# Attention and feed-forward in one program: scores of two pairs of heads in a row, three work banks

## The reference

```python
q = (layernorm(layernorm_plain(x)) @ Wq).reshape(b, 112, 16, 64)   # then q * (1 + side) + side
k, v = split(layernorm(ctx) @ Wkv)                                  # each 375 x 16 heads x 64
attn = softmax(einsum('bihd,bjhd->bhij', q, k) / 8)
x = x + tanh(g_x) * (einsum('bhij,bjhd->bihd', attn, v).reshape(b, 112, 1024) @ Wout)
h = gelu(bitlinear(layernorm_plain(x), w1, b1))                     # bitlinear: rmsnorm, rounding to
x = x + tanh(g_f) * bitlinear(h, w2, b2)                            # 127 steps a row, ternary weights
```

## Time and profile before

| | us |
|---|---|
| median of 3 runs (1168.94 to 1169.98) | 1169.59 |
| the profiled execution | 1169.56 |
| its span | 1167.3 |
| PE busy | 1105.4 (95%) |
| ACT busy | 976.1 (84%) |
| DVE busy | 934.5 (80%) |
| POOL busy | 767.9 (66%) |

### The profile page before, as it was taken

One profiled execution on the slowest core, in us unless ns is written; L12 is line 12 of the kernel. 1 busy time (PEld: TensorE's weight loads), 2 busy tenths in 40 slices (PEclk: granted clock), 3 DMA queues, 4 the chain that ended last, 5 costly groups with the idle time before them and its releaser, 6 DMA issues.

```text
span 1167.3 us, 32324 instructions
## 1 busy us (share of the span) xinstructions
PE 1105.4 (95%) x12170; PEld 746.9 (64%) x12170; DVE 934.5 (80%) x1980; ACT 976.1 (84%) x1866; POOL 767.9 (66%) x835
## 2 busy tenths in 40 slices
...
GB/s 267 72 97 114 107 110 102 102 103 96 96 116 96 111 100 108 97 99 106 99 112 93 108 92 117 94 111 99 104 99 102 107 106 109 95 94 89 98 93 14
DMA packets 381208, 120.57 MB, mean 103 GB/s; under 512 B 354848, under 2 KB 379904, under 8 KB 381056
## 3 DMA queue, kind: packets, MB, share of 16 engines
...
...
## 4 chain that ended last, share of the span: by engine, by line
PE 76%; DVE 8%; issue 5%; ACT 4%; DVEq 3%; POOL 2%; DMA 1%; POOLq 1%; ACTq 0%
PE work L737 16%; PE work L738 15%; PE work L739 15%; PE ps_s L756 10%; PE ps_o L737 3%; PE ps_o L738 3%; PE ps_o L739 3%; PE work L819 3%; DVEq L621 2%; PE work L850 2%; PE work L844 2%; PE work L810 2%; ACT prob L520 1%; DVE qs L629 1%; DVE attn L594 1%
## 5 line engine op out<-in xcount | busy, mean ns | idle before, releaser
L361 POOL TENSOR_TENSOR pn<-prob,pn 112x750 f16<-112x750 f32 x256 | 405.0, 1592 | 213.4 <-DVE pn L667 148.4
L520 ACT ACTIVATE prob<-ps_s,neg_max 112x375 f32<-112x375 f32 x512 | 265.3, 572 | 73.0 <-DVE neg_max L660 70.4
L660 DVE TENSOR_REDUCE neg_max<-ps_s 112x2 f32<-112x750 f32 x256 | 239.4, 935 | 66.7 <-PE ps_s L756 66.7
L737 PE MATMUL work<-z,wkv_h 128*128 128x375 f16 x512 | 167.6, 327 | 7.8 <-POOL z L382 6.6
L737 PE MATMUL ps_o<-v_h,pt 128*128 128x65 f16 (+1 forms) x1536 | 164.9, 195 | 7.4 <-DMA pt<-pn 7.4
L739 PE MATMUL work<-z,wkv_l 128*128 128x375 f16 x512 | 166.4, 325 | 0.0
L738 PE MATMUL work<-z,wkv_h 128*128 128x375 f16 x512 | 166.0, 324 | 0.0
L738 PE MATMUL ps_o<-v_l,pt 128*128 128x65 f16 (+1 forms) x1536 | 165.1, 193 | 0.0
L739 PE MATMUL ps_o<-v_h,pt 128*128 128x65 f16 (+1 forms) x1536 | 164.7, 193 | 0.0
L737 PEld LDWEIGHTS ps_o<-v_h,pt 128*128 128x128 f16 (+1 forms) x1536 | 143.7, 97 | 24.2 <-DMA pt<-pn 9.2
L738 PEld LDWEIGHTS ps_o<-v_l,pt 128*128 128x128 f16 (+1 forms) x1536 | 142.8, 99 | 14.8
...
## 6 DMA issues: line engine op xcount, KB each, us to landing
...
pt<-pn SPq DMA_TRANSPOSE x256, 3.2
...
```

The lines of the kernel that those rows point to most:

```text
L361: g.tensor_tensor(pn[p % PBUF][:, 1, :, 0:SK], prob[:, p % 2], pn[p % PBUF][:, 0, :, 0:SK], ALU.subtract).then_inc(p_lo, 1)
L520: i = a.activation(prob[:, p % 2, h, :], ps_s[0:SQ, h, 0:SK], ACT.Exp, bias=neg_max[:, h:h + 1])
L660: v.tensor_reduce(neg_max[:, :], ps_s[0:SQ, 0:2, 0:SK], X, ALU.max, negate=True).then_inc(max_ready, 1)
L737: t_.matmul(dst, sh, mh, start=(n == 0), stop=False)
```

## The change

- `ps_s` has four banks, two for even and two for odd pairs; `neg_max` four columns. S of a pair waits for E of two pairs back (`exp_done >= g - 1`).
- `ps_o` has one bank, four heads at a time; `normalise_heads` runs four times an item (`N0` to `N3`), each on four heads, and `A` of every even pair waits for the last of them.
- `work` has three banks.
- The lists are new. On PE the S steps stand mostly in twos: S0 S1, S2 S3, S4 S5, S6 S7. On ACT, `GE` is followed by KH5, ZF0, SQ, ZF1 and only then E6. POOL's list is the same round, begun at another point.
- x is loaded by a step of its own, `LX`; `LD` loads ctx and, for item 1, the rest as before.
- `ot_h` and `ot_l` become one array `ot`; `pn` and `pt` are picked by the running pair number g (the same buffers, as eight pairs go round four buffers twice).

```diff
-WORK_BANKS = 4
+WORK_BANKS = 3
 ORDER["PE"] = [
-    ("K5", 0), ("K7", 0), ("V00", 0), ("A4", -1), ("S0", 0), ("V01", 0), ("A5", -1), ("V02", 0),
-    ("S1", 0), ("K0", 1), ("Q1", 0), ("A6", -1), ("S2", 0), ("OO0", -1), ("XT", -2), ("K1", 1),
-    ("A7", -1), ("K2", 1), ("V10", 0), ("ZX", 1), ("S3", 0), ("V11", 0), ("A0", 0), ("F0", -2),
-    ("K3", 1), ("S4", 0), ("OO1", -1), ("F1", -2), ("K4", 1), ("HT", -3), ("A1", 0), ("S5", 0),
-    ("WO", -1), ("V12", 0), ("Z1", 2), ("Q0", 1), ("S6", 0), ("F2", -3), ("Z0", 2), ("K6", 1),
-    ("A2", 0), ("A3", 0), ("S7", 0),
+    ("Z1", 1), ("V02", 0), ("K7", 0), ("V00", 0), ("A4", -1), ("S0", 0), ("S1", 0), ("OO0", -1),
+    ("A5", -1), ("K6", 0), ("V01", 0), ("Q1", 0), ("A6", -1), ("ZX", 1), ("S2", 0), ("S3", 0),
+    ("K1", 1), ("K0", 1), ("A7", -1), ("V10", 0), ("K2", 1), ("V11", 0), ("K3", 1), ("S4", 0),
+    ("S5", 0), ("OO1", -1), ("XT", -2), ("A0", 0), ("K4", 1), ("A1", 0), ("HT", -3), ("Q0", 1),
+    ("F1", -2), ("V12", 0), ("F0", -2), ("WO", -1), ("K5", 1), ("S6", 0), ("S7", 0), ("Z0", 2),
+    ("F2", -3), ("A2", 0), ("A3", 0),
 ]
 FIRST["PE"] = [
-    ("Z0", 0), ("Z1", 0), ("ZX", 0), ("K0", 0), ("K2", 0), ("K1", 0), ("Q0", 0), ("K4", 0),
-    ("K3", 0), ("K5", 0), ("K6", 0), ("S0", 0), ("Z0", 1), ("V00", 0), ("Z1", 1), ("V01", 0),
...
+    ("Z0", 0), ("Z1", 0), ("ZX", 0), ("K1", 0), ("K0", 0), ("K3", 0), ("K4", 0), ("K2", 0),
+    ("Q0", 0), ("Z0", 1), ("K5", 0), ("Z1", 1), ("K7", 0), ("S0", 0), ("S1", 0), ("Q1", 0),
+    ("S2", 0), ("V00", 0), ("S3", 0), ("V02", 0), ("V01", 0), ("K6", 0), ("S4", 0), ("ZX", 1),
...
 ORDER["ACT"] = [
...
+    ("PH0", 0), ("VH01", 0), ("E1", 0), ("QF1", 0), ("ZXF", 1), ("XR", -2), ("KH1", 1), ("KH0", 1),
+    ("E2", 0), ("VH10", 0), ("E3", 0), ("KH2", 1), ("PH2", 0), ("VH11", 0), ("KH3", 1), ("LNW", 2),
+    ("OH1", -1), ("E4", 0), ("KH4", 1), ("PH4", 0), ("QF0", 1), ("E5", 0), ("VH12", 0), ("GE", -2),
+    ("KH5", 1), ("ZF0", 2), ("SQ", -2), ("ZF1", 2), ("E6", 0), ("VH02", 1), ("PH6", 0), ("E7", 0),
+    ("KH7", 1), ("VH00", 1), ("HR", -2), ("OH0", 0), ("E0", 1), ("KH6", 1),
...
 ORDER["DVE"] = [
...
+    ("M0", 0), ("KL7", 0), ("VL00", 0), ("PH7", -1), ("OT0", -1), ("N2", -1), ("M1", 0), ("KL6", 0),
+    ("VL01", 0), ("PH1", 0), ("M2", 0), ("BA", 2), ("BB", 2), ("KL1", 1), ("M3", 0), ("KL0", 1),
+    ("VL10", 0), ("BS", 2), ("KL2", 1), ("N3", -1), ("VL11", 0), ("KL3", 1), ("M4", 0), ("XTE", -2),
+    ("OT1", -1), ("PH3", 0), ("KL4", 1), ("HTE", -3), ("M5", 0), ("HE1", -2), ("N0", 0), ("HE0", -2),
+    ("PH5", 0), ("VL12", 0), ("X1", -1), ("XST", -1), ("M6", 0), ("KL5", 1), ("HMX", -2), ("YE", -3),
+    ("SC1", -1), ("M7", 0), ("N1", 0), ("VL02", 1), ("SC2", -2),
 ]
 FIRST["DVE"] = [
...
+    ("BA", 0), ("BB", 0), ("BS", 0), ("WKL", 0), ("BA", 1), ("KL1", 0), ("BB", 1), ("KL0", 0),
+    ("BS", 1), ("WQL", 0), ("KL3", 0), ("KL4", 0), ("KL2", 0), ("WVL", 0), ("KL5", 0), ("M0", 0),
...
 ORDER["POOL"] = [
...
+    ("PL7", -2), ("PL0", -1), ("PL1", -1), ("ZXS", 0), ("HQ", -4), ("XQ", -3), ("QS1", -1), ("LNA", 1),
+    ("PL2", -1), ("PL3", -1), ("PL4", -1), ("PL5", -1), ("RM1", -2), ("QS0", 0), ("RM2", -3), ("ZS0", 1),
+    ("PL6", -1), ("ZS1", 1), ("XB", -2),
...
 FIRST["SP"] = [
...
+    ("LD", 1), ("LX", 1), ("LD", 2), ("LX", 2), ("T0", 0), ("T1", 0), ("T2", 0), ("LD", 3),
...
-        ps_s = st.enter_context(nc.psum_tensor("ps_s", [P, 2, HALF], F32))
-        ps_o = st.enter_context(nc.psum_tensor("ps_o", [P, 2, HALF], F32))
+        ps_s = st.enter_context(nc.psum_tensor("ps_s", [P, 4, HALF], F32))
+        ps_o = st.enter_context(nc.psum_tensor("ps_o", [P, 1, HALF], F32))
...
-                sp.dma_start(x_in[:], x[b]).then_inc(x_loaded, 16)
...
+                if name == "LX" and b > 0:
+                    sp.wait_ge(ctx_normed, b)
+                    sp.dma_start(x_in[:], x[b]).then_inc(x_loaded, 16)
...
+            def normalise_heads(b, quarter):
+                n, heads = H // 4, ps_o[0:SQ, 0, 0:4 * VW].rearrange("p (h e) -> p h e", e=VW)
+                inv = row_inv[:, n * quarter:n * (quarter + 1)]
+                dve.wait_ge(pv_done, b * PAIRS + 2 * (quarter + 1))
...
             def score(b, p):
                 g = b * PAIRS + p
-                if g > 0:
-                    pe.wait_ge(exp_done, g)
+                if g > 1:
+                    pe.wait_ge(exp_done, g - 1)
...
-                        i = t_.matmul(ps_s[0:SQ, h, 0:SK], q[r, p, :], k[r, p, :], start=(n == 0), stop=(n == 2))
+                        i = t_.matmul(ps_s[0:SQ, 2 * (p % 2) + h, 0:SK], q[r, p, :], k[r, p, :], start=(n == 0), stop=(n == 2))
...
-                if p % 4 == 0 and b * PAIRS + p > 0:
-                    pe.wait_ge(o_normed, 2 * b + p // 4)
+                if p % 2 == 0 and b * PAIRS + p > 0:
+                    pe.wait_ge(o_normed, 4 * b + p // 2)
```

More of the change, by code:

```diff
@@ L189, in build @@
         RC = IC * RING // 2
-        ot_h, ot_l = (stage[:, RC * i:RC * (i + 1)].bitcast(F16).rearrange("p (c q) -> p c q", c=IC) for i in range(2))
+        ot = stage[:, 0:2 * RC].bitcast(F16).rearrange("p (h a c q) -> p h a c q", h=2, a=2, c=IC // 2)
         x1_b2 = stage[:, 2 * RC:2 * RC + 4 * D].rearrange("p (s d) -> p s d", s=4)
@@ L219, in build @@
         q_h, q_l = sb("q_h", [P, IC, SQ], F16), sb("q_l", [P, IC, SQ], F16)
-        neg_max, row_inv = sb("neg_max", [SQ, 2]), sb("row_inv", [SQ, H])
+        neg_max, row_inv = sb("neg_max", [SQ, 4]), sb("row_inv", [SQ, H])
         prob = sb("prob", [SQ, 2, 2, SK])
@@ L360, in split_p @@
                 pool.wait_ge(p_hi_act if p in CAST_ACT else p_hi, CAST_COUNT[b, p])
-                g.tensor_tensor(pn[p % PBUF][:, 1, :, 0:SK], prob[:, p % 2], pn[p % PBUF][:, 0, :, 0:SK],
+                buf = pn[(b * PAIRS + p) % PBUF]
+                g.tensor_tensor(buf[:, 1, :, 0:SK], prob[:, p % 2], buf[:, 0, :, 0:SK],
                                 ALU.subtract).then_inc(p_lo, 1)
@@ L475, in step @@
                         act.wait_ge(full[BANK["WO", t]], USE["WO", t])
-                    a.activation(ot_h[:, 4 * half:4 * half + 4, columns(b)],
+                    a.activation(ot[:, half, 0, :, columns(b)],
                                  work[:, BANK[job], 0:4 * SQ].rearrange("p (c q) -> p c q", c=4), ACT.Identity).then_inc(o_hi, 1)
@@ L519, in step @@
                     for h in range(2):
-                        i = a.activation(prob[:, p % 2, h, :], ps_s[0:SQ, h, 0:SK], ACT.Exp, bias=neg_max[:, h:h + 1])
+                        i = a.activation(prob[:, p % 2, h, :], ps_s[0:SQ, 2 * (p % 2) + h, 0:SK], ACT.Exp, bias=neg_max[:, 2 * (p % 2) + h:2 * (p % 2) + h + 1])
                     i.then_inc(exp_done, 1)
@@ L528, in step @@
                     if g >= PBUF:
-                        act.wait_ge(turned[p % PBUF], 16 * (g // PBUF))
-                    a.activation(pn[p % PBUF][:, 0, :, 0:SK], prob[:, p % 2], ACT.Identity).then_inc(p_hi_act, 1)
+                        act.wait_ge(turned[g % PBUF], 16 * (g // PBUF))
+                    a.activation(pn[g % PBUF][:, 0, :, 0:SK], prob[:, p % 2], ACT.Identity).then_inc(p_hi_act, 1)
                 if name == "XR":
@@ L586, in lo @@
                                        op0=ALU.mult, op1=ALU.subtract).then_inc(evacuated[BANK[job]], 1)
-            def normalise_heads(b, half):
-                n, heads = H // 2, ps_o[0:SQ, :, 0:4 * VW].rearrange("p b (h e) -> p b h e", e=VW)
-                inv = row_inv[:, n * half:n * (half + 1)].rearrange("p (b h) -> p b h", b=2)
-                dve.wait_ge(pv_done, b * PAIRS + 4 * (half + 1))
-                v.reciprocal(inv, heads[:, :, :, DH])
+            def normalise_heads(b, quarter):
+                n, heads = H // 4, ps_o[0:SQ, 0, 0:4 * VW].rearrange("p (h e) -> p h e", e=VW)
+                inv = row_inv[:, n * quarter:n * (quarter + 1)]
+                dve.wait_ge(pv_done, b * PAIRS + 2 * (quarter + 1))
+                v.reciprocal(inv, heads[:, :, DH])
                 dve.drain()
-                v.tensor_tensor(attn[:, half * HALF:(half + 1) * HALF].rearrange("p (b h d) -> p b h d", b=2, d=DH),
-                                heads[:, :, :, 0:DH], inv.unsqueeze(3).broadcast_to([SQ, 2, n // 2, DH]),
+                v.tensor_tensor(attn[:, quarter * D:(quarter + 1) * D].rearrange("p (h d) -> p h d", d=DH),
+                                heads[:, :, 0:DH], inv.unsqueeze(2).broadcast_to([SQ, n, DH]),
                                 ALU.mult).then_inc(o_normed, 1)
@@ L659, in step @@
                     dve.wait_ge(scored, g + 1)
-                    v.tensor_reduce(neg_max[:, :], ps_s[0:SQ, 0:2, 0:SK], X, ALU.max, negate=True).then_inc(max_ready, 1)
+                    v.tensor_reduce(neg_max[:, 2 * (p % 2):2 * (p % 2) + 2], ps_s[0:SQ, 2 * (p % 2):2 * (p % 2) + 2, 0:SK], X, ALU.max, negate=True).then_inc(max_ready, 1)
                 if name[0:2] == "PH":
@@ L665, in step @@
                     if g >= PBUF:
-                        dve.wait_ge(turned[p % PBUF], 16 * (g // PBUF))
```

(3 more changed lines are left out.)

32 lines of the change are left out of this document (15 added, 17 removed), and 79 rows, old and new, of the table CAST_ACT.

## The result

The changed kernel takes 1191.84 us (1190.73 to 1192.34), the kernel before 1169.26 (1168.55 to 1169.98): a ratio of 1.0191, interval 1.0179 to 1.0204. It is slower by 22.6 us, where 13.5 less was forecast. The profiled execution has a span of 1190.0 us, 22.7 more than before, so the trace carries the whole difference.

The account below looks back on a forecast made before the run. TensorE was taken as the path, busy 991 of 1000 us in the middle. -28 - 12 + 21 + 3 + 5 = -11, or -16 with 17 us of present waits; the middle, -13.5, gave 1156 us, range 1136 to 1171.

Parts of the forecast that it names:

- E6: ScalarE's Exp step of pair 6: walked as coming behind the reload of the Exp table, 0.93 us to the next start.
- Part 1, the junctions: TensorE's score steps: 123 junctions between runs of S go, at 0.23 us each, -28 us, bounds 0 and -28.
- Rival (b): TensorE's score steps: the junctions don't merge, so the -28 falls away, 1184 us; chance 0.12.
- Part 2, the wait at S1: TensorE before S1: waits 0.75 us for an Exp step behind the table load, in 28 items, +21 us.
- Rival (a): TensorE before S1: the wait does not occur or hides, so the +21 falls away, 1135 us; chance 0.20.
- "most of the present 12 us of waits" go: TensorE's existing waits: most stop when its steps shift, since their places are gone, -12 us.
- chains without slack: LNA chain to HT, Q0 to F0, N1 to A4: 0.1 us an item together, +3 us, between 0 and +15.
- "PE waits for VectorE's ot or k_l": Profile after: a sign that the forecast is wrong, if TensorE waits for these instead; no size given.
- Part 3, one head bank: VectorE's normalising: four steps of 256 columns for two of 512, 0.8 us more per item, covered by idle time.
- Part 4, the start: Start of the kernel: x of item 1 lands near 32, Q0 begins near 37, +5 us, between +2 and +9.
- (c): GpSimd's LNA chain: 1 us later than walked, it holds the three work banks and costs 30 us, 1186; chance 0.16.
- (d): ScalarE's table change before Exp costs twice its row, 1.28 us more, 28 times, 36 us, 1192; chance 0.02.

Follow-up runs that it names:

- The two partial orders: Changed kernel with ScalarE's late Exp step moved ahead: 1190.66 us; with x early, that step and the transposes moved forward, some evacuations back: 1193.67 us.

## Why the prediction was wrong

- **Part 1, the junctions: right.** -28 was forecast for the kernel; in the 30 items of the middle it is -27.1, or -25.7 with the V step more. Three of four pairs parted again put 19.5 us of steps back, 17.0 of time. Rival (b) falls.
- **Part 2, the wait at S1: right in place and cause, a little high.** 0.75 us was forecast, the median is 0.68; 16.2 us in the middle for +21. Rival (a) falls.
- **Part 2, "most of the present 12 us of waits" go, plus 3 for chains without slack: this is the step that failed.** The old waits did go. But the same late E6 holds two more resources, which the sum put at nothing: K6 waits for KL7 (0.42 us in nearly every item, 11.0 in all), and A7 for the transpose behind PH7 and PL7 (8.8 in all). I had walked ScalarE's list against TensorE's up to S1 and stopped at the first consumer; the stretch of VectorE's list that begins with VL02, behind VH02 and E6, and runs by SC2 and M0 to KL7, VL00 and PH7 was not walked, and T7's landing was not looked at. The text had "PE waits for VectorE's ot or k_l" among its signs of being wrong, and that sign is there (k_l 6.2 us). The chains I named as slackless (LNA to HT, Q0 to F0) cost next to nothing: HT waits 1.6 us in the middle. A4, whose slack I had put at 0.1 us, waits 6.5, 4.0 of it once, for the queue of the transposes; in 18 of 30 items it starts 0.10 us behind N1's end. Measured: +34.2 of waits for a forecast of -12 + 21 + 3 = +12. That is 22 of the 36 us between forecast and result; the start gives 9 (13.6 for +5), the junctions 2, and 2.5 the middle that I took between two sums for the present waits (12 or 17; the same reckoning as in the table gives 16.0).
- **Part 3, one head bank: right.** The product of 256 columns takes 0.42 us for 0.45, its reciprocal 0.17 for 0.20, so a new item costs VectorE 0.6 us more for 0.8. What one bank costs TensorE is inside A4's waits.
- **Part 4, the start: every time was right but the sum.** Landing 32.0, K2 33.0, Q0 36.5 for 37. The sum of +5 took TensorE to have caught up but for 5 us by 47; measured is +9.6 at S0 of item 0 and +13.6 at S0 of item 1. What I had as the bound of +9, the clock going down, happened. The other part was missed: the statistics finished late feed LNA, LNA's power ran at 3.08 us beside WQL, and LNW stands ahead of KH4 and KH2. By the run with x early 8.0 us of the total are x's (8.8 at S0 of item 1 in the traces). The rest is the new FIRST order; WQL early takes back 3.4 of the total, by a way that is not clear. The moved LX also holds T4 of item 1, at the seam of FIRST and ORDER. And "in the steady state nothing changes" holds for x, not for the queue it stands on: by the median T4, T5 and T7 take longer to land in every round, and A7 waits for T7.
- **Rivals (c) and (d).** (c), LNA on GpSimd, came near the result (1186) by the wrong mechanism. It was put as windows of 1.5 to 2 us in which one late step costs every item, and that form is right: the late step was E6, not LNA. (d) falls, though its 1192 is the time measured, by chance: the rows show the load of 1.28 us 0.02 behind the end of ZF1, and Exp 0.01 behind the load. By the Trainium skill, "ScalarE: Activation LUTs", section "What ACT_TABLE_LOAD costs", a change of table is about 2.66 us; the trace shows half of that on the path here too. The 1194 us that the prediction works out from it lie near the result by chance as well: they need a wait of 2.1 us at S1, and it is 0.68. What the load costs the kernel depends on its place all the same: about 1 us in the old order, 24 in the new.
- **Cover.** In the middle nothing was bound by VectorE's time: it is busy 825 of 1000 us, and what moved the result was which of its steps came first.

So the gain went into one late step, E6 behind the table load, with three consumers behind it. What the runs show: without the load 24 us go, nearly all of S1's wait and about half of K6's, but only 2.5 of A7's 8.8; with E6's chain, VectorE's list and the evacuations all brought forward and x early, the waits at S1, K6 and A7 are gone and the time is below that of the kernel before. The two partial orders show less: each of them served some consumers and made another step late by its own edit, so they don't tell what serving one consumer alone is worth. Open are the 2.4 us of WQL, why T7 lands later in the changed kernel, and how the start's loss divides between the idle time and the lower clock, which no run parted.
